# Attention scores in four 64x64 array tiles, adapter scores over 128 tokens at once, V transposes in the next step

## The reference, cut to what matters

```
z   = agg_w(b) @ x(b) + agg_b            # per batch, 64x64 mix from a small MLP
q, k, v = split(z @ w_attn.T)            # 32 heads of 32 channels
q, k = rope(q), rope(k)
y   = softmax(causal(q k.T / sqrt(32))) v          # within a batch: 64 x 64 scores a head
a   = gating * softmax(q ak.T / sqrt(1024)) av     # 10 adapter tokens, ak and av from adapter_wte
x1  = x + (y + a) @ w_proj.T
out = x1 + base and LoRA layer(grouped conv of x1)  # router, top 2 of 8 experts
```

## Time and profile before

| | |
|---|---|
| Time, median of 3 runs | 1267.33 us (1265.48 to 1268.0) |
| Profiled execution: span from first to last instruction | 1264.7 us |
| TensorE busy | 1235.9 us, 98% |
| TensorE weight loads busy | 1063.3 us, 84% |
| VectorE / ScalarE / GpSimd busy | 733.2 / 383.4 / 105.8 us |
| Projections of q, k, v (L828) | 782.8 us |
| Scores / adapter scores / V transposes (L777 / L788 / L868) | 62.3 / 19.6 / 21.0 us |

### The profile page before, as it was taken

How to read it: one execution, slowest core, us unless ns; L and a number is a source line. 1 busy time by engine, 2 the same in 40 slices (tenths; PEclk the granted TensorE clock), 3 DMA queues, 4 the chain that set the end, 5 groups by cost and what they waited for, 6 DMA issues and landing times.

```text
span 1264.7 us, 20870 instructions
## 1 busy us (share of the span) xinstructions
PE 1235.9 (98%) x7940; PEld 1063.3 (84%) x7940; DVE 733.2 (58%) x1447; ACT 383.4 (30%) x699; POOL 105.8 (8%) x52
## 2 busy tenths in 40 slices
PE   8799999999999999999999999799999999999998
PEld 6688888888888888888888887699999999999998
DVE  5965856857666676776767759544333333343432
ACT  4433343433443434435334355311000000011100
POOL 2600000000000000000000004400000000110001
PEclk9999999999999999999999999899999999999999
DMA  6311101001001001001001303722222222222221
GB/s 223 108 39 37 40 9 66 8 17 58 8 17 58 12 12 58 17 8 65 10 9 67 141 11 107 236 84 83 100 94 99 106 83 83 87 95 83 84 83 50
DMA packets 52703, 83.98 MB, mean 66 GB/s; under 512 B 5546, under 2 KB 38846, under 8 KB 51518
## 3 DMA queue, kind: packets, MB, share of 16 engines
q1 hardware_dynamic: 52670, 83.52, 19.3%
HBM read 58.33 MB, written 25.17 MB: 66 GB/s over the span
## 4 chain that ended last, share of the span: by engine, by line
PE 90%; DVE 5%; issue 2%; ACT 1%; DMA 1%; SPq 0%; DVEq 0%; ACTq 0%
PE psum L828 39%; PE psum L909 16%; PE psum L882 13%; PE psum L777 5%; PE psum L894 4%; PE psum L818 2%; PE psum L803 2%; PE psum L929 2%; PE psum L868 1%; DVE m_z L339 1%; PE psum L858 1%; PE psum L788 1%; DVE z L274 1%; PE psum L796 1%; PE psum L811 1%
## 5 line engine op out<-in xcount | busy, mean ns | idle before, releaser
L828 PE MATMUL psum<-z,w_hi 128*128 128x512 f32 x1536 | 482.4, 395 | 4.3 <-DVE m_z L339 2.5
L828 PEld LDWEIGHTS psum<-z,w_hi 128*128 128x128 f32 x1536 | 285.0, 189 | 62.6 <-issue 2.6
L828 PE MATMUL psum<-z,w_lo 128*128 128x512 f32 x768 | 300.4, 391 | 0.0
L828 PEld LDWEIGHTS psum<-z,w_lo 128*128 128x128 f32 x768 | 144.9, 189 | 31.2
L1051 ACT ACTIVATE a_kbd<-a_kr 32x512 f32<-32x512 f32 x128 | 80.6, 629 | 234.9 <-DVE a_kr L1153 233.8
L1167 DVE TENSOR_TENSOR a_prob<-psum,a_mask 128x512 f32<-128x512 f32 x64 | 43.9, 687 | 107.5 <-PE psum L777 106.8
L909 PE MATMUL psum<-f_wfhi,f_chi 128*128 128x388 f32 (+1 forms) x384 | 93.8, 339 | 1.9 <-DVE f_osb L1292 1.5
L909 PE MATMUL psum<-f_wfhi,f_clo 128*128 128x388 f32 (+1 forms) x384 | 93.6, 338 | 0.0
L909 PE MATMUL psum<-f_wflo,f_chi 128*128 128x388 f32 (+1 forms) x384 | 93.5, 338 | 0.0
L882 PE MATMUL psum<-f_wphi,f_yhi 128*128 128x512 f32 x256 | 81.8, 401 | 1.4 <-DVE f_ylo L1221 1.4
L754 POOL TENSOR_TENSOR f_x1b<-f_x,f_bbase 128x1024 f32<-128x1024 f32 x16 | 48.5, 3033 | 389.9 <-DVE f_osb L1294 383.0
(11 more groups left out here) (150 smaller groups left out, 1694.6 us busy)
## 6 DMA issues: line engine op xcount, KB each, us to landing
w_st<-in_wqkvT SPq DMA_DIRECT2D x8, 1536.0 KB, 6.9
m_x<-in_x SPq DMA_DIRECT2D x16, 512.0 KB, 4.2
y_scratch<-a_ysb SPq DMA_DIRECT2D x32, 256.0 KB, 2.3
f_yst<-y_scratch SPq DMA_DIRECT2D x16, 512.0 KB, 4.2
f_xt<-in_x SPq DMA_DIRECT2D x16, 512.0 KB, 3.4
x_scratch<-f_x SPq DMA_DIRECT2D x16, 512.0 KB, 2.6
_x<-x_scratch SPq DMA_DIRECT2D x128, 64.0 KB, 2.4
out<-f_osb SPq DMA_DIRECT2D x16, 512.0 KB, 2.6
```

What stands on the lines that cost most here:

```text
L828: mm = pe.matmul(dst, w[:, c, x, :], zs, start=(c == 0 and i == 0), stop=(c == KC - 1 and i == 2))
```

## The change

`kbd` holds K for two heads of the same half of the rows side by side (128 rows, 2 x 64 columns) instead of four. A score matmul contracts over 64 rows (two heads), streams 128 columns, and has its own quarter of the array: row half t by column half b. Row half t writes the bank bS[t], so a bank now holds a head pair of all 8 batches. Both banks are complete only at the end of the stage. Adapter scores take 128 tokens as stationary operand in one matmul, and are issued ahead of the scores. The V transposes of a unit leave the end of its step and come after the scores of the next step. pT is laid out by head pair, and the value matmuls wait for both of its copies at once.

```diff
-        kbd = sb("kbd", [P, UB, GH, NC])
+        kbd = sb("kbd", [P, UB, 2, NC])
+        sb("kbd_pad", [P, UB, 2, NC])
...
-        pT = [sb(f"pT{t}", [P, 2, 2, P]) for t in range(2)]
+        pT = [sb(f"pT{t}", [P, UP, P]) for t in range(2)]
...
-            def attend_scores(m):
+            def attend_scores(m, groups):
                 pe.wait_ge(rotated[Q_], m + 1)
                 pe.wait_ge(kbd_set, m + 1)
                 wait(pe, aT_copied, m)
                 wait(pe, pT_copied, 2 * m)
-                for s in range(UP):
-                    for b in range(2):
-                        mm = pe.matmul(bS[s // 2][NC * b:NC * b + NC, (s % 2) * GH * NC:(s % 2 + 1) * GH * NC],
-                                       qr[:, (2 * s + b) * NC:(2 * s + b + 1) * NC],
-                                       kbd[:, 2 * s + b, :, :].rearrange("p h k -> p (h k)"), start=True, stop=True)
-                    if s % 2:
-                        mm.then_inc(scores, 1)
-
-            def attend_ascores(m, groups):
                 wait(pe, ashifted, m)
                 pe.wait_ge(akbd_set, groups)
                 for i in range(UP):
+                    mm = pe.matmul(bAD[:, i * GH * NA:(i + 1) * GH * NA], qr[:, i * P:(i + 1) * P],
+                                   akbd[:].rearrange("p h a -> p (h a)"), start=True, stop=True)
+                mm.then_inc(ascores, 1)
+                for s in range(UP):
                     for b in range(2):
-                        mm = pe.matmul(bAD[NC * b:NC * (b + 1), i * GH * NA:(i + 1) * GH * NA],
-                                       qr[:, (2 * i + b) * NC:(2 * i + b + 1) * NC],
-                                       akbd[:].rearrange("p h a -> p (h a)"), start=True, stop=True)
-                mm.then_inc(ascores, 1)
+                        for t in range(2):
+                            heads = slice(2 * HD * t, 2 * HD * (t + 1))
+                            mm = pe.matmul(bS[t][NC * b:NC * b + NC, s * 2 * NC:(s + 1) * 2 * NC],
+                                           qr[heads, (2 * s + b) * NC:(2 * s + b + 1) * NC],
+                                           kbd[heads, 2 * s + b, :, :].rearrange("p h k -> p (h k)"),
+                                           start=True, stop=True)
+                            if s == UP - 1 and b == 1:
+                                mm.then_inc(scores, 1)
...
                 pe.wait_ge(vbd_set, m + 1)
+                pe.wait_ge(pT_copied, 2 * m + 2)
                 for s in range(UP):
-                    if s % 2 == 0:
-                        pe.wait_ge(pT_copied, 2 * m + s // 2 + 1)
...
-                                           vbd[:, s, b, hp, :], pT[s // 2][:, s % 2, hp, NC * b:NC * b + NC],
+                                           vbd[:, s, b, hp, :], pT[hp][:, s, NC * b:NC * b + NC],
...
+            def turn_values(m):
+                pe.wait_ge(vT_copied, m + 1)
+                for i in range(UP):
+                    tr = pe.transpose(bV[:, i * P:(i + 1) * P], vT[:, i * P:(i + 1) * P], ident[:])
+                tr.then_inc(v_tr, 1)
...
                 if att:
-                    attend_scores(n - 1)
-                    attend_ascores(n - 1, groups)
+                    attend_scores(n - 1, groups)
+                    turn_values(n - 1)
                 wait(pe, turned[K_], n)
...
                 if u == 0:
                     pe.wait_ge(akv_copied, g + 1)
-                pe.wait_ge(vT_copied, n + 1)
-                for i in range(UP):
-                    tr = pe.transpose(bV[:, i * P:(i + 1) * P], vT[:, i * P:(i + 1) * P], ident[:])
-                tr.then_inc(v_tr, 1)
-                if u == 0:
                     pe.matmul(bAD[:, AVS:AVS + P], asel[:], akv[:, P:2 * P], start=True, stop=True)
                     pe.matmul(bAD[:, AKT:AKT + NA], akv[:, 0:P], afold[:], start=True, stop=True).then_inc(ak_tr, 1)
...
             m = NG * NU - 1
-            attend_scores(m)
-            attend_ascores(m, NG)
+            attend_scores(m, NG)
+            turn_values(m)
...
                 for h in range(GH):
-                    cp = act.activation(kbd[HD * h:HD * (h + 1), :, h, :],
+                    cp = act.activation(kbd[HD * h:HD * (h + 1), :, h % 2, :],
                                         kr[HD * h:HD * (h + 1), :].rearrange("p (b k) -> p b k", k=NC), ACT.Copy)
```

More of the change, by code:

```diff
@@ L1004, in attend_copies @@
                     act.wait_ge(p_tr, 2 * m + t + 1)
-                    act.activation(pT[t][:].rearrange("p s h q -> p (s h q)"), src[:], ACT.Copy).then_inc(pT_copied, 1)
+                    act.activation(pT[t][:].rearrange("p s q -> p (s q)"), src[:], ACT.Copy).then_inc(pT_copied, 1)
             def y_copy(m):
```

## The result

The changed kernel takes **1284.4 us** (median of 4 runs, 1283.78 to 1285.85); the kernel before took 1266.99 in its 4. The ratio is 1.0143 (95% interval 1.0131 to 1.0156): **slower by 17.4 us**. The forecast was 1270.0 and its range ended at 1279, so both missed: the direction came out as the sum had it, the size did not. The profiled execution has a span of 1281.8 us, 17.1 more than before.

A forecast was written before the change was run, and what follows sets the result against it. TensorE's queue was taken as the bound: -13.2 us from 30 units, +6.0 and +9.8 for stalls on Q and adapter keys, +0.1 for the last two units, +2.7 in all, giving 1270.0 us, range 1257 to 1279.

The forecast's parts named there:

- The stages: TensorE's adapter scores 1.00, scores 1.07, V transposes 0.40: 2.47 us against 2.91, 0.44 us a unit less.
- Four tiles at once: Score matmuls: all four 64x64 tiles run together, 8 rounds of 0.116 us, stage 0.72 us less than before.
- The 128-token adapter scores: Adapter stage: eight 128-column weight loads do not hide, 1.00 us instead of 0.54, costing 0.46 us a unit.
- Stall (b): Adapter scores at u = 1 wait for the new group's adapter keys: 1.22 us eight times, +9.8 us.
- VectorE's start: First score operation at T0 + 2.19, 0.47 us later; T0 is TensorE done with value matmuls and array shape changed.
- ScalarE's `vbd` copy: Copy after the moved V transposes ends at T0 + 4.30, 0.06 us before the exponential queued behind it is ready.
- The sum: TensorE savings in 30 units, stalls on Q and adapter keys, last two units: +2.7 us in total.
- Stall (a): Adapter matmuls at the group's end wait for Q's rotation on VectorE: 0.86 us seven times, +6.0 us.
- Term (c): Last two units, waiting on VectorE: -0.2 and +0.3 us, +0.1 in the sum, uncertain by 1 us.
- A': Rival, scores: four tiles run, but a round takes 0.139 us; +6 us, 1276 us; chance 13%.
- B: Rival, scores: pass order limits the array to two tiles at a time, stage 1.96 us; 1298 us; chance 15%.
- C: Rival, adapter scores: 128-column loads hide, stage stays 0.55 us; 14.4 us off, 1255.6 us; chance 17%.

The follow-up runs named there:

- e4: Kernel before with only the scores in four 64x64 tiles, their waits put ahead of the last V transpose: 1251.4 us.
- e6: Kernel before with only the adapter scores changed to 128 tokens a matmul, still after the scores: 1278.8 us.
- e2: Changed kernel with ten 128x128 transposes of a constant ahead of the wait on the adapter keys at u = 1: 1274.2 us.
- e5: Kernel before with only the wait on the adapter keys moved ahead of the scores, giving eight gaps of 1.2 us: 1276.7 us.
- e11: Changed kernel without the four tiles: scores, kbd and pT as in the kernel before, all else of the change kept: 1305.6 us.
- e8: e5 with the V transposes moved behind both score stages of the next step: 1271.8 us.
- e12: e1 with 64-token adapter scores and, on VectorE, Q rotated ahead of the low part of the next K weights: 1243.5 us.
- e1: Changed kernel with scores ahead of adapter scores, and waits for Q and kbd ahead of the previous unit's last value matmul (u = 0: afold matmul): 1254.6 us.
- e9: e4 with the wait on the adapter keys and one transpose of a constant ahead of the scores at u = 1: 1267.6 us, median of 10 runs.
- e7: e4 with the two small products that make the adapter keys put ahead of the V transposes at u = 0: 1248.9 us.

## Why the prediction was wrong, point by point

**Right.** The bound: TensorE's queue, in which 0.70 us saved a unit, 21 in 30 units, shows as 14.6 us (e4), and 0.46 added a unit as its full 13.8 (e6). The stages: 1.01, 1.04 and 0.38 where 1.00, 1.07 and 0.40 were worked out; period 21.65 where it said 21.67. Four tiles at once, which the earlier trace rows had suggested: the trace shows 32 starts in 1.04 us. The Trainium skill ("TensorE: Matmul & The Clock Gate", Part 3) has a strict start order, by which it would have been two tiles if both passes of a matmul stand side by side in the program, and 3.07 times for four row tiles, by which a round would be 0.139 (an estimate from that page's figure). The trace fits neither number: less the prediction's 0.05 for the first load and 0.09 for the change of shape, a round of four is (1.04 - 0.14) / 8 = 0.11. The records don't name the tile, so the order itself is not seen. The 128-token adapter scores at +0.46 (e6). Stall (b): 9.8 us in the sum, 9.8 in the waits, 8 times 1.22. VectorE's start at T0 + 2.17 for 2.19. ScalarE's `vbd` copy did not hold up anything.

**The failed step: the sum.** It priced each stall as idle time and nothing else, -13.2 + 6.0 + 9.8 + 0.1, and had no term for the clock. The earlier trace rows showed a granted clock of 9 in nearly every slice, and I took full speed for every stage of after too. What ran in its place: in five of eight windows behind the adapter keys' gap the clock was at 1.2 GHz for 3.4 to 6.9 us, 11.9 us in all. That this hangs on the gap is shown by e2 (gap filled, adapter matmuls in place, no fall at the eight places, -10.2 us); that the gap alone does not do it, by e5 (the same 9.8 us of gap, clock 1.00). That the adapter matmuls first behind it bring it on, also without the tiles, is shown by e11 against e8 (eight of eight against one of eight); that they are not enough either, by the seven gaps on Q in after (1.1 us, the same matmuls behind, no fall). The row that could have warned me is in the trace of before: its first 76 us, the mixing stage with its gaps above all, have a clock of 0.96.

```profile
0.00:76.00 76.00, 62.88 (x380) 0.96 0.45 154
```

**Stall (a), mis-sized.** 0.86 x 7 = 6.0 forecast, 7.2 measured: 1.1 six times and 0.64 once. Q's rotation ended on time, but in the six the matmul does not start 0.06 us later. Timeline of after at a group's end:

```profile
238.52 0.69 DVE L1152 TENSOR_TENSOR a_qr<-a_qr,a_rot 128x512 f32<-128x512 f32 x1
...
239.58 1.06 PE L779 MATMUL psum<-a_akbd,a_qr 128*128 128x40 f32 x8 [1.11 <-DVE a_qr L1152]
```

Q is there at 239.21, the first matmul starts at 239.58: 0.37. Behind the wait on Q stand five more waits in TensorE's own order (kbd, aT, pT, the shift, the keys). They are long fulfilled, and before they were passed while the V transposes ran; in after they come one by one once Q's is released. The line views of 239.2 to 239.6 show three instructions of TensorE's sequencer, in its load queue (PEldq), between Q's end and the first load at 239.55:

```profile
L66 PEldq ALU_OP  x2: 36/36/36, 239.2 to 239.3; - x2
L777 PEldq EVENT_SEMAPHORE  x1: 51/51/51, 239.5 to 239.5; - x1
```

At the seventh group's end the other waits stand ahead of Q's and are passed at 699.4 to 699.6. No such instruction comes between Q's end (700.64) and the first matmul, and it starts 0.06 us later, as forecast:

```profile
699.95 0.69 DVE L1152 TENSOR_TENSOR a_qr<-a_qr,a_rot 128x512 f32<-128x512 f32 x1
...
700.70 1.09 PE L779 MATMUL psum<-a_akbd,a_qr 128*128 128x40 f32 x8 [0.64 <-DVE a_qr L1152]
```

The same sort of time shows once more at the loop's turn from u = 1 to u = 2, 0.3 us in five steps (1.3 us, put down to "issue"). In e12 and e1 the waits stand ahead of a matmul that runs anyway.

**Term (c).** The last two units: +0.1 forecast, the wait at L796 grew from 3.1 to 5.2 us. It was called uncertain by 1 us.

**The rivals.** A', B and C are refuted by periods of single parts (e4, e6). What happened was none of them: it is the forecast's own case with a second price on its stalls. Without the clock the terms as measured come to about +7.6 on the span, so slower would have held without it, at about 1275 us. My first two theories of that price fell in turn: the gap alone (e5), and the tiles behind it (e11).

**Open.** Why one gap brings the clock down and the next, with the same instructions, does not: after's fourth, fifth and seventh gap left it at 1.00, and e9's count varies from run to run. The counts 0, 1, 3, 5 and 8 of eight rank the kinds of work behind the gap in one profile each and give no rule; 5 against 8 has no second witness in the clocks of the single runs. No kernel had the tiles alone first and the 128-token adapter scores second behind a gap, so their shares in after's falls aren't parted; no kernel had 64-token adapter scores first behind a gap either, so their order and their width aren't parted. And what makes the gaps on Q harmless in after, what stands ahead of them or their 0.1 us less, was not tried; e8, where the V transposes no longer stand ahead of the key gap, has one fall where e5 has none.

## What to carry to other kernels

An early wait for the newest input can cost twice on a TensorE-bound kernel: its idle time, and then the clock, as here where small matmuls like these adapter scores came first behind it; put work that does not need the input first (e1: -30 us by order and the place of waits), or make the input earlier (e7, e12). Time each part of a change alone: here the tiles were worth -14.6 us, the wider adapter matmuls cost +13.8 and the order with the place of the waits about 30, and together they looked like one slow idea. Where a stall is added to a kernel whose clock row is all 9s, give the clock a term in the range.

## What the runs showed of the hardware that was not expected

- Idle time of 1.2 us was followed by half clock or not, depending on what came after it: none of eight with 256-column matmuls first (e5), eight of eight with 40-column matmuls first (e11), and each of these falls lasted 3.4 or 6.8 us at 1.2 GHz. Idle time of 1.1 us with the same 40-column matmuls behind it and value matmuls ahead brought none in seven (after) and three in seven (e2).
- Filling an idle wait with transposes of a constant made a kernel 9 to 10 us faster, although the wait itself ended no sooner (e2 against after).
- Four 64x64 tiles ran side by side: 16 f32 matmuls of 128 columns (32 instructions) in 1.04 us, the change of shape included, about 0.11 us for a round of four.
- Waits that were already fulfilled were not free behind one that was not: 0.34 to 0.37 us from Q's end to the first matmul at the six group ends where they stand behind it, 0.06 at the seventh, where they stand ahead.
